# GpSimd adds up its own products in the closing program, before TensorE's identity sums

## The reference

```
def _L0_xattn_ref(q, k, v):          # q = layernorm(x), k = v = ctx_1024
    hd = D // NHEADS                 # 256 // 16 = 16
    qh = q.reshape(B, S, NHEADS, hd)
    kh = k.reshape(B, S, NHEADS, hd)
    vh = v.reshape(B, S, NHEADS, hd)
    scores = jnp.einsum('bsqd,bskd->bsqk', qh, kh) / math.sqrt(hd)
    scores = jnp.where(tril(NHEADS, NHEADS), scores, -1e18)
    attn = jax.nn.softmax(scores, axis=-1)
    return jnp.einsum('bsqk,bskd->bsqd', attn, vh).reshape(B, S, D)
```

## Time and profile before

| | us |
|---|---|
| median of 3 runs | 810.05 (809.73 to 810.14) |
| the profiled execution | 811.71 |
| its span in the trace | 809.9 |
| closing program, from POOL's last products of the batches to the end | about 720 to 809.9 |

### The profile page before, as it was taken

One profiled execution on the slowest core, in us unless ns is written; L12 is line 12 of the kernel. 1 busy time (PEld: TensorE's weight loads), 2 busy tenths in 40 slices (PEclk: granted clock), 3 DMA queues, 4 the chain that ended last, 5 costly groups with the idle time before them and its releaser, 6 DMA issues.

```text
span 809.9 us, 16213 instructions
## 1 busy us (share of the span) xinstructions
PE 746.5 (92%) x5733; PEld 528.2 (65%) x5733; DVE 601.1 (74%) x1227; ACT 401.2 (50%) x760; POOL 493.0 (61%) x458
## 2 busy tenths in 40 slices
PE   8788999999998999999999989999999999898996
PEld 6555565755575656666666757675766565478996
DVE  3544555457768896889778886888787959699984
ACT  5123555455555556555736564656565555552111
POOL 5000000031975889687958796879867896986763
PEclk9998999999999999999999999999999999999999
DMA  5886666866686668567756775677666770100101
GB/s 186 111 109 105 79 80 86 137 86 87 86 137 79 92 87 136 68 86 115 91 99 84 112 91 93 84 116 93 97 86 101 97 112 8 60 8 14 34 14 39
DMA packets 47981, 70.55 MB, mean 87 GB/s; under 512 B 4897, under 2 KB 22578, under 8 KB 47922
## 3 DMA queue, kind: packets, MB, share of 16 engines
q1 hardware_dynamic: 46898, 69.52, 57.4%
q10 hardware_dynamic: 1024, 0.26, 0.2%
HBM read 14.98 MB, written 4.19 MB: 24 GB/s over the span
## 4 chain that ended last, share of the span: by engine, by line
PE 63%; DVE 13%; DMA 10%; ACT 7%; issue 4%; POOL 1%; SPq 1%; ACTq 0%; DVEq 0%; POOLq 0%
PE misc L525 19%; PE exp_bank L525 16%; PE max_bank L525 10%; DMA stack_k<-k_lo 9%; PE acc_bank L525 8%; PE sum_bank L525 7%; DVE neg_max L1225 3%; DVE head_out L1237 3%; ACT probs L950 2%; ACT x_in L910 1%; PE misc L575 1%; ACT values L903 1%; SPq L456 1%; DVE prod L360 1%; PE misc L642 1%
## 5 line engine op out<-in xcount | busy, mean ns | idle before, releaser
L950 ACT ACTIVATE probs<-exp_bank 128x512 f32<-128x512 f32 x320 | 185.9, 594 | 202.8 <-PE sum_bank L525 109.6
L1225 DVE TENSOR_REDUCE neg_max<-max_bank 128x1 f32<-128x512 f32 (+1 forms) x192 | 130.2, 683 | 108.9 <-PE max_bank L525 107.9
L1603 POOL TENSOR_TENSOR prod<-head_probs,ctx_sb 128x256 f32<-128x256 f32 (+1 forms) x100 | 181.8, 1851 | 2.2 <-POOL head_probs L1598 0.5
L525 PE MATMUL max_bank<-stack_k,stack_q 96*128 96x384 f32 (+3 forms) x512 | 155.2, 364 | 15.0 <-DMA stack_k<-k_lo 8.1
L525 PE MATMUL exp_bank<-stack_q,stack_k 97*128 97x384 f32 (+3 forms) x512 | 149.8, 354 | 15.8 <-ACT probs L950 14.9
L315 POOL TENSOR_TENSOR prod<-x1n,ctx_sb 128x256 f32<-128x256 f32 (+1 forms) x104 | 158.2, 1553 | 4.6 <-ACT x1n L910 4.6
L1537 POOL TENSOR_TENSOR ln_var<-ln_mv,eps 128x4 f32<-128x4 f32 x21 | 4.5, 212 | 198.1 <-DVE ln_mv L1211 198.1
L525 PEld LDWEIGHTS exp_bank<-stack_q,stack_k 97*128 97x128 f32 x512 | 83.3, 192 | 48.3 <-ACT probs L950 23.2
L1225 DVE TENSOR_REDUCE seg_max<-max_bank 128x4 f32<-128x512 f32 x128 | 86.8, 684 | 37.5 <-PE max_bank L525 36.5
L525 PEld LDWEIGHTS max_bank<-stack_k,stack_q 96*128 96x128 f32 x512 | 85.8, 198 | 22.5 <-DMA stack_k<-k_lo 9.8
L525 PE MATMUL acc_bank<-probs,values 128*32 128x512 f32 (+3 forms) x1024 | 96.4, 447 | 0.9 <-ACT probs L950 0.9
(11 more groups left out here) (183 smaller groups left out, 1372.6 us busy)
## 6 DMA issues: line engine op xcount, KB each, us to landing
stack_q<-q_hi SPq DMA_DIRECT2D x64, 256.0 KB, 5.0
stack_k<-k_hi SPq DMA_DIRECT2D x64, 256.0 KB, 9.5
stack_q<-q_lo SPq DMA_DIRECT2D x32, 256.0 KB, 7.0
stack_k<-k_lo SPq DMA_DIRECT2D x32, 256.0 KB, 10.7
x_in<-in_x SPq DMA_DIRECT2D x9, 512.0 KB, 6.0
ctx_sb<-in_ctx SPq DMA_DIRECT2D x32, 128.0 KB, 3.1
x<-in_x SPq DMA_DIRECT2D x7, 512.0 KB, 10.3
out<-y_sb SPq DMA_DIRECT2D x5, 512.0 KB, 3.2
```

Source lines behind the costliest of these rows:

```text
L525: return nc.tensor.matmul(*args, **kw)
L950: nc.scalar.activation(probs[:, (UNITS * g + n) % PTR, :], exp_bank[n % 2][:, :], ACT.Exp, scale=SCALE).then_inc(exp_done, 1)
L1225: vec.tensor_reduce(o, v, axis=AX_X, op=ALU.max, negate=True).then_inc(max_taken, 1)
L1603: last = gp.tensor_tensor(pv_prod[:, COFF[j]:COFF[j + 1]].rearrange("p (q d k) -> p q d k", q=4, k=keys), head_probs[:, 4 * j:4 * j + 4, N ...
```

## The change

POOL adds its own products up before it signals them. For the scores it adds dimensions 12, 13 to 14, 15 (320 elements) and then 12 to 13 (160 elements), so that TensorE sums one dimension of POOL's in place of four. For the values it adds, for both key groups, the upper two keys to the lower two (256 and 128 elements), then one to the other (128 and 64), so that TensorE sums one key of each of POOL's groups in place of four. `own` signals a semaphore with the instruction and waits for it on POOL.

```diff
 def end_score_sums(u):
-                dims = list(range(*POOL_DIMS))
+                dims = [POOL_DIMS[0]]
 def end_value_sums(u):
-                    for k in range(4):
+                    for k in range(1 if j in POOL_KEYS else 4):
                         last = mm(value_sum_bank[:, C - width:C], ident[:, :],
                                   end_prod_pv[:, KOFF[j] + k * width:KOFF[j] + (k + 1) * width],
-                                  start=(j == 0 and k == 0), stop=(j == CHUNKS - 1 and k == 3), skip_group_check=True)
+                                  start=(j == 0 and k == 0), stop=(j == CHUNKS - 1), skip_group_check=True)
 def end_pool_scores(u):
-                end_score_products(gp, u, POOL_DIMS).then_inc(end_qk_pool, 1)
+                own(end_score_products(gp, u, POOL_DIMS))
+                d0, d1 = POOL_DIMS
+                own(gp.tensor_tensor(end_prod_qk[:, d0:d0 + 2, :], end_prod_qk[:, d0:d0 + 2, :],
+                                     end_prod_qk[:, d0 + 2:d1, :], ALU.add))
+                gp.tensor_tensor(end_prod_qk[:, d0, :], end_prod_qk[:, d0, :], end_prod_qk[:, d0 + 1, :],
+                                 ALU.add).then_inc(end_qk_pool, 1)
 def end_pool_values(u):
                 for j in POOL_KEYS:
                     last = end_value_products(gp, u, j)
+                own(last)
+                for keys in (2, 1):
+                    for j in POOL_KEYS:
+                        width = keys * (NH - 4 * j) * HD
+                        v = end_prod_pv[:, KOFF[j]:KOFF[j] + width]
+                        last = gp.tensor_tensor(v, v, end_prod_pv[:, KOFF[j] + width:KOFF[j] + 2 * width], ALU.add)
+                    if keys == 2:
+                        own(last)
                 last.then_inc(end_pv_pool, 1)
```

## The result

The changed kernel takes 819.33 us (817.57 to 820.03, 4 runs) against 810.1 before: ratio 1.0097, interval 1.0074 to 1.012, or 7.9 us slower. The two medians alone are 9.2 us apart; I go by the ratio, since the kernel before had medians of 811.3 to 811.6 us when it was timed beside the experiments. The forecast was 2.5 us slower, with a range to 816.

What follows compares the result with a forecast made beforehand. PE was taken as the bound in the second half only, by a few tenths of a us per tile, DVE right behind. POOL's longer chain +1.9 and the clock +0.6 made +2.5 on 810.05: 812.5 us, range 807.5 to 816.

Steps and rivals of the forecast that it cites:

- u = 5: Schedule step for tile 6's score sum: start 775.65 against 771.4, end 779.35, tile 6's maxima at 779.4 against 776.03.
- Rival B: Additions ahead of the score sums are cheap or hidden, DVE stays the bound: -4.3 us, 805.8; chance 0.18.
- PE starts at 738.5: Tile 3's score sum: PE starts after POOL's additions at 738.5, not at 736.63.
- Starts there: Tile 4's score sum: PE starts when POOL's additions end at 753.05, 2.2 us late, and ends at 756.8.
- GpSimd's own waits for VectorE's products: Each addition beside a DVE product may wait out one of some 0.4 us; upper bounds 2.2 and 2.6 us.
- The price of the additions: On POOL: 1.42 us per score chain, six times, and 1.82 per value chain, seven times; 21.2 us in all.
- My lower bound for the values: POOL's value additions cost at least 0.90 us per tile, with no instruction cheaper than 0.19.
- The clock: One more fall of PE's clock that matters, before tile 6's sum, two thirds absorbed by DVE's order: +0.6 us.
- Rival C: PE's clock falls in most tiles, five falls at 1.6 us, some hidden: +5.5 us, 815.5; chance 0.14.
- The context's load: Last context tile's load follows POOL's 758.35, giving tile 4's exponential at about 762.5, just in time.
- POOL busy over 9 tenths: Sign that the forecast is right: POOL busy over 9 tenths in the slices from 740 to 795.

Runs made afterwards that it cites:

- e3: The change with TensorE's shorter sums kept and all GpSimd additions dropped, so products are left out of the result: 807.81 us, 0.9952 to the kernel before.
- e4: The change with all GpSimd additions made but TensorE still summing all four dimensions and keys: 821.57 us, 1.0122 to the kernel before.
- e7: The change with TensorE summing VectorE's twelve score dimensions first and GpSimd's one last: 815.35 us, 1.0042 to the kernel before.
- e5: The change with idle matmuls on TensorE ahead of its wait for GpSimd, 22 at tile 4 and 36 at tile 6: 816.63 us, 1.0069 to before.
- e6: The change with the next context tile's load released by GpSimd's value products, not its additions: 819.26 us, 1.0094 to the kernel before.
- e9: The kernel before plus additions in idle slots only: both score levels at tiles 5 and 7, first value level at tiles 6 and 7; 809.24 us, 0.9969.
- e12: The kernel before, without any addition, with GpSimd's four score dimensions summed last: 808.72 us, 0.9967 to the kernel before.
- e15: e9 and e12 together, additions only in idle slots and GpSimd's score part summed last: 808.44 us, 0.9963 to the kernel before.
- e2: The change with GpSimd's value additions only, scores summed as before: 812.64 us, 1.0011 to the kernel before.
- e8: The change with the edits of e6 and e7 together: 813.93 us, 1.0034 to the kernel before.
- e13: The change without its second addition for the scores, values keeping both levels: 815.4 us, 1.0051 to the kernel before.
- e10: The change with the first level of additions only, TensorE summing two of GpSimd's dimensions and keys: 812.03 us, 1.0006 to the kernel before.

## Why the prediction was wrong, by its own steps

- **The step that failed** is *u = 5*: "PE's score sum of tile 6 starts 775.65", "ends 779.35, and maxima of tile 6 follow at 779.4". It started at 778.47, took 5.95 us and not 3.7, and the maxima came at 784.45. I had 10.65 us from the maxima of tile 5 to those of tile 6, and it took 14.7. The start was late by terms that I had too small (what blocks GpSimd, the price of the additions), and the length was the clock, which I had put at 0.6.
- **The direction and the larger mechanism held.** I forecast that additions ahead of each sum in GpSimd's chain eat the saving: e3 and e4 show it from both sides, and e7 gives 4.5 us back by moving them behind most of the sum. Rival B's price for hidden additions, -4.3, was nearly e3's -3.9.
- **"PE starts at 738.5"** for tile 3: 738.52. **"Starts there"** for tile 4, 753.05: 753.75. Tile 5: 762.65 by my steps (both done at 762.6, and 0.05 to PE's start), 764.30 measured; there the additions had ended at 761.73, and PE was late from tile 4's transposes. **"Starts 775.65"** for tile 6: 778.47. Maxima of tile 6 **"at 779.4"**: 784.45. The miss grows from tile to tile: 0, 0.7, 1.7, 2.8, then 5.
- **The term that was mis-sized most: GpSimd's own waits for VectorE's products.** I counted it for VectorE's score products only. At tiles 4 and 6 and once more before the last values, a GpSimd instruction waits out a 1024-element value product, 0.9 us each time (1.38 for 0.52, twice, and 1.15 for 0.20). I had the upper bound in hand ("may wait out one DVE product of some 0.4 us") with the wrong product in it: the one that stands there takes 1.22. The 2.7 us are read from the trace; no run takes these blocked instructions out alone.
- **The price of the additions.** 0.87 and 0.52 alone for my 0.78 and 0.46, 1.96 and one wait for my 1.82: 6 x 1.53 + 7 x 2.03 = 23.4 us in place of 21.2. (My lower bound for the values, 0.90, is 0.86 by its own terms; nothing rests on it.)
- **The clock.** I counted 0.6 us for the fall at tile 6, "two thirds absorbed". The sum took 5.95 us for 3.6, VectorE waited 4.6 us for it, and e5 gives back 2.3: little or nothing was absorbed, since VectorE had come to its wait. Rival C was wrong in its extent: one new fall in the tiles behind tile 3, not five.
- **The context's load,** "just in time": it took 3.96 us from issue to landing, not 2.1, and PE waited 2.7 us for tile 4's transposes behind it. Why it took longer stays open: SP issues a store of the result 0.38 us behind it in the kernel before too, where it landed in 2.1. It was a delay, but e6 shows that the end did not hang on it.
- **POOL busy over 9 tenths** was wrong: 16.77 of 20.9. I had added its own work to a stretch that gets longer. The bound is the round from engine to engine.

Together the three blocked instructions (2.7), the clock (2.3 for 0.6) and the prices (2.2) are 6.6 us, of which 5.4 were needed to get from 2.5 to 7.9; their overlap is not resolved.

## What to carry to other kernels

Work moved to a second engine is worth what its successor waits for now, and costs what stands behind it in the *round* of waits: look for slots in which the engine idles (here e9's tiles) and add only there. Before shortening a sum, sum the late producer's part last; here that alone (e12, 2.7 us) gained as much as the best placing of the additions (e9, 2.5 us), and both together (e15, 3.0 us) can't be told from either. And count for every instruction moved to GpSimd the longest VectorE product that can stand beside it, not the one that stands there today.

## What the hardware showed that I had not expected

GpSimd's instructions of 2 elements also wait out VectorE's two-input product (1.15 us for 0.20), so small work is no safer than large. It was the same instruction, L1634 ahead of the last values, 1.15 to 1.17 us long in the change, e2, e5 to e8 and e13, and never over 0.6 in the kernels with no or one level of value additions. GpSimd's additions lie on one line, 0.17 us + 2.2 ns for each element (worked out from 0.87 at 320 and 0.52 at 160; by it 256 and 128 elements back to back are 1.18, and e10 has 1.14), where the rows of before had given 0.46 at 160 between a subtraction of 256 and an operation of 2 elements. The granted clock fell in the sum after PE had stood still 5.37 us, and not in the one after 3.32 us at tile 4; before, 2.39 us had been enough at tile 3. In e9 1.90 us had been enough at tile 3 (0.57 in 736.5 to 740.5). So the length of a stop alone did not decide it here.
